# First loads, late value groups and half key products in the prologue of an attention and expert layer

## The reference

```python
q = x @ Wq + bq; k = x @ Wk + bk; v = x @ Wv + bv
q, k, v = (to_heads(q), to_heads(k), to_heads(v))        # 8 heads of 64
scores = jnp.einsum('bdsh,bdth->bdst', q, k) / SCALE
weights = jax.nn.softmax(scores, axis=-1)
feats = jnp.einsum('bdst,bdth->bdsh', weights, v)
x = _layernorm(x + (feats.reshape(B, S, F) @ Wo + bo))
# router: sigmoid(x @ w_gate), top 6 of 64 experts, places by a running count
# x_disp: the rows of x scattered to (expert, place), zero where no token stands
up = jnp.einsum('ecd,edh->ech', x_disp, w_up)
out_r = jnp.einsum('ech,ehd->ecd', silu(g_r) * v_r, w_down)
x = _layernorm(x + shared + routed)
```

## Time and profile before

| what | value |
|---|---|
| median of 3 runs | 1390.62 us (1387.7 to 1397.6) |
| the profiled execution | 1395.11 us, of which the span of the trace is 1393.3 us |
| busy share of the span | PE 92%, DVE 73%, ACT 65%, POOL 48% |
| prologue | 0 to 150.8 us in the trace |
| attention's first scores | 159.2 us |
| mean granted clock of TensorE | 0.974 of full speed |

### The profile page before, as it was taken

How to read it: one execution, slowest core, us unless ns; L and a number is a source line. 1 busy time by engine, 2 the same in 40 slices (tenths; PEclk the granted TensorE clock), 3 DMA queues, 4 the chain that set the end, 5 groups by cost and what they waited for, 6 DMA issues and landing times.

```text
span 1393.3 us, 24378 instructions
## 1 busy us (share of the span) xinstructions
PE 1280.9 (92%) x8129; PEld 1068.5 (77%) x8129; DVE 1017.0 (73%) x1879; ACT 901.2 (65%) x1639; POOL 664.8 (48%) x662
## 2 busy tenths in 40 slices
PE   6999799999999999999999999996678999999596
PEld 4888599899899899799799799796456767767332
DVE  4623488789799899799799789796445677677376
ACT  5411398878688688688688688686114666666242
POOL 0002122235636636636636636546363888888511
PEclk9999899999999999999999999998798999999899
DMA  6049966112423424324334333334455999997597
GB/s 232 0 186 353 344 215 217 55 37 86 136 70 129 130 86 137 105 86 137 112 95 129 121 102 127 108 107 140 157 204 171 335 353 346 347 359 274 208 419 303
DMA packets 155754, 252.78 MB, mean 181 GB/s; under 512 B 18660, under 2 KB 98916, under 8 KB 153201
## 3 DMA queue, kind: packets, MB, share of 16 engines
q1 hardware_dynamic: 130144, 192.19, 40.9%
q0 software_dynamic: 20992, 50.38, 9.5%
q10 hardware_dynamic: 4496, 8.65, 1.7%
HBM read 118.95 MB, written 134.33 MB: 182 GB/s over the span
## 4 chain that ended last, share of the span: by engine, by line
PE 66%; issue 12%; DMA 6%; SPq 4%; DVE 4%; POOL 4%; ACT 3%; another core or an unknown queue 2%; POOLq 0%; DVEq 0%; ACTq 0%
PE pv_acc L1256 13%; PE slot L1237 13%; PE slot L1224 12%; PE slot L1119 8%; PE slot L1333 4%; PE slot L1283 4%; PE misc L1170 4%; PE pv_acc L1119 4%; DMA got<-y_hbm 3%; SPq L397 3%; DVE rows_lo L1059 2%; ACT rows_hi L783 2%; PE slot L1355 1%; DMA moved<-scaled 1%
## 5 line engine op out<-in xcount | busy, mean ns | idle before, releaser
L740 ACT ACTIVATE p_hi<-slot 128x512 fp32r<-128x512 f32 x512 | 279.8, 596 | 108.6 <-PE slot L1224 86.4
L590 POOL TENSOR_TENSOR p_lo<-prob,p_hi 128x512 fp32r<-128x512 f32 x128 | 165.1, 1290 | 363.4 <-ACT prob L742 356.9
L1237 PE MATMUL slot<-k_stack,q_stack 128*128 128x512 f32 x1024 | 300.8, 416 | 8.5 <-DMA q_stack<-q_hbm 8.5
L753 ACT ACTIVATE prob<-prob,row_min 128x1024 f32<-128x1024 f32 x256 | 296.4, 1158 | 12.9 <-DVE prob L1035 12.9
L1014 DVE TENSOR_TENSOR p_lo<-slot,p_hi 128x512 fp32r<-128x512 f32 x384 | 251.3, 681 | 37.6 <-ACT p_hi L740 31.0
L1256 PE MATMUL pv_acc<-p_hi,v_pair 128*128 128x256 f32 x1024 | 265.6, 292 | 3.9 <-POOL p_lo L590 3.2
L1224 PE MATMUL slot<-ident,prob 128*128 128x128 f32 x2048 | 265.2, 272 | 1.2 <-ACT prob L753 1.2
L1256 PE MATMUL pv_acc<-p_lo,v_pair 128*128 128x256 f32 x1024 | 255.1, 282 | 0.0
L1224 PEld LDWEIGHTS slot<-ident,prob 128*128 128x128 f32 x2048 | 230.8, 140 | 1.7 <-DVE prob L1035 1.6
L1256 PEld LDWEIGHTS pv_acc<-p_hi,v_pair 128*128 128x128 f32 x1024 | 193.0, 189 | 18.0 <-issue 8.6
L1256 PEld LDWEIGHTS pv_acc<-p_lo,v_pair 128*128 128x128 f32 x1024 | 192.8, 188 | 11.7 <-issue 3.3
(11 more groups left out here) (142 smaller groups left out, 2092.4 us busy)
## 6 DMA issues: line engine op xcount, KB each, us to landing
disp_hbm<-zeros SPq DMA_DIRECT2D x64, 512.0 KB, 5.5
rows<-disp_hbm SPq DMA_DIRECT2D x64, 512.0 KB
y_hbm<-zeros SPq DMA_DIRECT2D x48, 512.0 KB
got<-y_hbm SPq DMA_DIRECT2D x16, 1536.0 KB, 11.9
q_stack<-q_hbm SPq DMA_DIRECT2D x128, 128.0 KB
up_w<-in_L_ffn_w_up SPq DMA_DIRECT2D x64, 256.0 KB
down_w<-in_L_ffn_w_down SPq DMA_DIRECT2D x32, 256.0 KB
q_hbm<-q_hi SPq DMA_DIRECT2D x8, 512.0 KB, 2.6
```

Of the source, the lines that this page charges most:

```text
L590: e.tensor_tensor(p_lo[1][:, 2:4, :], prob[:, m % 2, :, (4 * u + 2) * P:(4 * u + 4) * P], p_hi[1][:, 2:4, :].bitcast(F32), ALU.subtract).t ...
L740: e.activation(p_hi[b][:, two, :], view[:, two, :], ACT.Copy).then_inc(a_phi, 1)
L753: e.activation(keys, keys, ACT.Exp, bias=row_min[:, me % 2, j, 1:2], scale=-1.0, accum_out=row_sum[:, me % 2, j, half:half + 1]).then_inc( ...
L1237: made = e.matmul(slot[:, n * BANK:(n + 1) * BANK], qs[:, part, j * P:(j + 1) * P], k_stack[:, ms % H, keys], start=part == 0, stop=part == 1)
```

## The change

It has four parts. The first loads of q_stack (heads 0 and 1) are issued ahead of the zeroes, with a wait for the last query product (q_stack lies where the query weights were), and 24 of the zeroes stand in the prologue and 40 in the loop, where 32 and 32 did. The last two value groups are made behind the scores of steps 0 and 1, and DVE's part of them is placed between its steps 0 to 3. The first three key products are made by halves: the first half of all three, then the second half of all three. And PE, ACT and DVE wait for the constants alone (`constants_in`) ahead of attention, while PE waits for the value parts ahead of the first product with v_pair, in step 7; SP and POOL keep `prologue_over`. Three small tiles (row_min, row_sum, row_inv) move out of the memory that the prologue uses.

```diff
+        V_LATE = 2
         takes = [("k", n) for n in range(8)]
-        takes += [("q", n) for n in range(8)] + [("v", g) for g in range(NS)]
+        takes += [("q", n) for n in range(8)] + [("v", g) for g in range(NS - V_LATE)]
         for s in range(LAST + LAG):
             takes += ([("turn", s - LAG)] if s >= LAG else []) + ([("scores", s)] if s < LAST else [])
+            takes += [("v", NS - V_LATE + s)] if s < V_LATE else []
...
+        def constants_in(e):
+            e.wait_ge(g_const, 5)
+            e.wait_ge(d_fill, 16)
+            e.wait_ge(d_once, 32)
...
# SP
-            for g in range(E // 2):
-                e.dma_start(disp_pieces[g], zero_row).then_inc(d_zero, 16)
...
+            e.wait_ge(p_q, 8)
             load_q(0)
             load_q(1)
+            for g in range(Z_EARLY):
+                e.dma_start(disp_pieces[g], zero_row).then_inc(d_zero, 16)
             prologue_over(e)
...
-                if s < E // 2:
-                    e.dma_start(disp_pieces[E // 2 + s], zero_row).then_inc(d_zero, 16)
+                if s < E - Z_EARLY:
+                    e.dma_start(disp_pieces[Z_EARLY + s], zero_row).then_inc(d_zero, 16)
...
# DVE
+            for g in range(NS - V_LATE):
+                add_v(g)
+                if g < NS - V_LATE - 1:
+                    low_v(g)
+            constants_in(e)
...
+                if s < V_LATE:
+                    low_v(NS - V_LATE - 1 + s)
+                    add_v(NS - V_LATE + s)
+                elif s == V_LATE + 1:
+                    low_v(NS - 1)
...
# PE
-            for n in range(8):
+            for half in range(2):
+                for n in range(3):
+                    project("k", n, 0, n, 0, (half,))
+            for n in range(3, 8):
                 project("k", n, n // 4, n % 4, 0)
...
+            for g in range(NS - V_LATE):
+                make_v(g)
+            constants_in(e)
...
                     made.then_inc(p_scores, 1)
+                    if s < V_LATE:
+                        make_v(NS - V_LATE + s)
...
+                    if rv == 0:
+                        e.wait_ge(a_vhi, 2 * NS)
+                        e.wait_ge(v_vlo, NS)
+                        e.wait_ge(g_vlo, NS)
```

More of the change, by code:

```diff
@@ L109, in build @@
         count_so_far = sb("count_so_far", [P, E], BF16, att)
+        row_min = sb("row_min", [P, 2, QT, 2], F32, att)
+        row_sum = sb("row_sum", [P, 2, QT, 2], F32, att)
+        row_inv = sb("row_inv", [P, QT], F32, att)
         pro = ExitStack()
@@ L128, in build @@
         q_stack = [sb(f"q_stack{i}", [P, 2, QC], F32R, att) for i in range(2)]
-        row_min = sb("row_min", [P, 2, QT, 2], F32, att)
-        row_sum = sb("row_sum", [P, 2, QT, 2], F32, att)
-        row_inv = sb("row_inv", [P, QT], F32, att)
         scaled = sb("scaled", [P, QC], F32, att)
@@ L300, in build @@
         y_pieces = y_hbm.rearrange("(g p t) (u n) -> g p (t u) n", p=P, t=2, u=2)
-        NZ = T * TOPK // (2 * P)
+        NZ, Z_EARLY = T * TOPK // (2 * P), 24
         bv_all = wo_sb[:, 0, :]
@@ L700, in scalar @@
                                  ACT.Copy).then_inc(a_vhi, 1)
-            prologue_over(e)
+            constants_in(e)
             def flip_x1(c, j):
@@ L896, in vector, with add_v @@
             e.wait_ge(d_bv, 16)
-            for g in range(NS):
-                vp = v_plain[g % 2]
+            def add_v(g):
                 e.wait_ge(p_v, g + 1)
@@ L902, in vector, with low_v @@
                     e.wait_ge(g_vlo, g - 1)
-                e.tensor_tensor(vp[:, :, :], slot_of_take("v", g)[:, :].rearrange("p (t n) -> p t n", t=2),
+                e.tensor_tensor(v_plain[g % 2][:, :, :],
+                                slot_of_take("v", g)[:, :].rearrange("p (t n) -> p t n", t=2),
                                 bv_all.unsqueeze(1).to_broadcast([P, 2, C]), ALU.add).then_inc(v_vadd, 1)
+            def low_v(g):
                 e.wait_ge(a_vhi, 2 * g + 2)
-                e.tensor_tensor(v_pair[:, 2 * g + 1, :, D:P], vp[:, 1, :].rearrange("p (h c) -> p h c", h=H),
+                e.tensor_tensor(v_pair[:, 2 * g + 1, :, D:P],
+                                v_plain[g % 2][:, 1, :].rearrange("p (h c) -> p h c", h=H),
                                 v_pair[:, 2 * g + 1, :, 0:D].bitcast(F32), ALU.subtract).then_inc(v_vlo, 1)
-            prologue_over(e)
+            for g in range(NS - V_LATE):
[3 more added lines that the diff above has]
+            constants_in(e)
             def add_resid(c, j):
@@ L1122, in three_products, with project @@
                     made.then_inc(done, 1)
-            def project(name, n, g, pair, w):
+            def project(name, n, g, pair, w, halves=(0, 1)):
                 slot = slot_of_take(name, n)
@@ L1135, in project @@
                 cols = slice(pair * P, (pair + 1) * P)
-                for half in range(2):
+                for half in halves:
                     four = slice((2 * g + half) * 4, (2 * g + half + 1) * 4)
@@ L1148, in tensor, with make_v @@
             e.wait_ge(v_wlo, KC + 2)
-            for g in range(NS):
+            def make_v(g):
                 wait_bank(e, ("v", g), 0)
```

## The result

The changed kernel takes 1388.28 us (median of 20 runs), the kernel before 1395.63 us in the same comparison (20 runs): a ratio of 0.9952, with a 95% interval of 0.9938 to 0.9966, so 6.7 us faster (4.7 to 8.7). The forecast was 12.4 us, to 1378.2 us. The kernel before has a median 5.0 us above the one of three runs on which the forecast was built, which is why ratios are used from here on. The two traces have spans of 1393.3 and 1387.9 us.

What follows compares the result with a forecast made beforehand. PE was taken to bound attention, so time won ahead of it would stay won. The terms, 5.15 + 10.8 - 3.6 = 12.4 us, taken from 1390.62 us gave 1378.2 us, with a range of 1371 to 1386.

Steps and rivals of the forecast that it cites:

- What bounds the kernel: In attention PE is busy throughout; time is won only where PE stands still or runs slowly ahead of it.
- Part 1: Start of the kernel: key products by halves fill PE's 4.22 us without work, gaining 5.15 us (4.5 to 5.8).
- Part 2: Ahead of attention: first loads and late value groups bring the first transposes 10.8 us earlier (10.3 to 11.3).
- Part 3: Step 8: head 2's load follows SP's large wait, Wo and three zeroes, so PE waits 3.6 us (2.7 to 4.7).
- the sum: Whole kernel: 5.15 + 10.8 - 3.6 = 12.4 us faster, to 1378.2 us.
- The rival of the clock: At step 8's new wait the clock halves, costing 2.7 us: 9.7 us gained, 1380.9 us; chance 0.14.
- The other three rivals: Head 2's load in time, 1374.6 us, 0.12; key product reading holds PE, 1382.2, 0.05; queue never catches up, 1403.4, 0.02.

Runs made afterwards that it cites:

- the kernel with the large wait: Changed kernel with all value groups ahead of attention and the large wait on PE, ACT and DVE as before the change; ratio 0.993 to the kernel before, 9.6 us faster.

## Why the prediction was wrong

*What bounds the kernel, and that a us won ahead of attention stays won*: right. Four kernels with leads of 7.9, 14.8, 17.9 and 18.2 us at the first head have 8.4, 14.8, 17.5 and 22.5 at the last expert, and their timed gains, 7.0, 12.4, 14.9 and 16.2, follow at 1 to 3 us less.

*Part 1, the halves*: forecast 5.15 (4.5 to 5.8), measured 6.3 in the two traces and 7.0 by the timed runs of that part alone (4.5 to 9.3). The steps were right, as the rows of the changed kernel show that answer to the earlier trace rows:

```profile
12.70 0.63 PE L1141 MATMUL slot<-x_hi,w_lo 128*128 128x512 f32 x1
...
13.13 0.63 PE L1141 MATMUL slot<-x_hi,w_hi 128*128 128x512 f32 x1
13.56 0.63 PE L1141 MATMUL slot<-x_lo,w_hi 128*128 128x512 f32 x1
...
13.98 0.56 PE L1141 MATMUL slot<-x_hi,w_lo 128*128 128x512 f32 x1
...
14.38 0.40 PE L1141 MATMUL slot<-x_hi,w_hi 128*128 128x512 f32 x1
14.61 0.40 PE L1141 MATMUL slot<-x_lo,w_hi 128*128 128x512 f32 x1
```

No gap follows the last matmul of product 0's first half (12.70), and 3 slow matmuls do, where I had 1 to 7; from 14.38 the distance is 0.23. They stand 0.40 to 0.43 us apart, as the score matmuls of the kernel before do at a granted clock of 0.50 (four in 1.71 us, 161.07 to 162.78). The windows of the start show 1.00, so that the half clock there is read from the distances alone. Nothing waits for the reading of the key products. PE free at 13.13 and not at 13.47 is 0.3 us of the difference, and 0.2 the smaller number of slow matmuls. The last 0.5 is in the pace: the fast matmuls up to the end of group 5 stand 0.2328 us apart in the trace before and 0.2317 in this one, and there are over 500. The other traces have 0.231 to 0.233, so that is scatter and no merit of the change. With group 5 ending anywhere from 131.85 to 134.92, the gain would be 4.6 to 7.7 us against this one trace of the kernel before; a range of 4.5 to 5.8 was too narrow for it.

*Part 2*: forecast 18.3 us from value group 5 to the first transposes and a gain of 10.8, measured 18.29 and 10.85 (17.11 less 6.26). The order of DVE's list and the durations in the earlier trace rows carried this without a fault.

*Part 3, what the change leaves in its place*: this is the term that failed, "PE waits for 3.6 us". The mechanism and its place were right, and the ends, 2.7 to 4.7, were too near. The wait measured 6.8 us, with 1.95 of slow clock behind it, which the sum had at nothing. SP's wait fell at 150.89, 17.6 behind the end of group 5, as forecast. Two prices behind it were wrong.

The first is the rate. I sent Wo and the zeroes through the queue at 385 GB/s, the rate of zeroes in a queue that has been full for long, so that they had moved 25.2 us behind the end of group 5, at 158.4. By the windows their 2.62 MB had moved at 160.6. Of these 2.2 us, 1.5 were lost in the first 2 us and the rest from 154.5 to 157.0. Why the queue was slow there is not shown. Wo met an empty queue, but it is also a load, and no run separates the two. The kernel before has a stretch in which its queue is not empty, the loads of q_stack end and Wo begins, and the rate falls to 248 and 260 there:

```profile
156.50:157.00 0.50, 0.00 (x0) 0.00 (x0) 0.00 (x0) 0.00 (x0) 0.00 (x0) 0.50 1.11 293
157.00:157.50 0.50, 0.00 (x0) 0.00 (x0) 0.00 (x0) 0.00 (x0) 0.00 (x0) 0.50 1.26 248
157.50:158.00 0.50, 0.00 (x0) 0.00 (x0) 0.00 (x0) 0.00 (x0) 0.00 (x0) 0.50 1.48 260
```

So even the trace before had a row that spoke against 385 GB/s for loads.

The second is the landing. I let the load be in 2.2 us behind the bytes ahead of it: 1.3 to move, and 1 for its semaphore, which no run separates. (At the 133 to 168 GB/s that the text names, 0.26 MB takes 1.6 to 2.0 and not 1.3; and 27.4 less 23.7 is 3.7, not 3.6.) It took 3.0, from 160.6 to 163.6. By the windows 2.88 MB, which is Wo, three zeroes and the load, had moved by about 161.3, and by the time the load was in, nearly 0.9 MB of the zeroes issued behind it had moved too. That fits engines that don't go in step, with a load that is in when the last of them has its share; but it is read from sums of bytes, and no run isolates it.

The estimate by the Trainium skill's fixed 2.0 us and 436 GB/s (DMA: Bandwidth & Descriptors, Anatomy of one DMA), a wait of 2.6 us, was further off still. The page gives that fit for a single transfer issued by GpSimd, and the trace disagrees with it for SP's transfers, which queue.

*The rival of the clock* held 0.14 as an alternative to a wait of 3.6 us. It was no separate case but belonged into the sum: with a wait of 6.8 us the clock fell, as in the earlier trace rows. In the traces with waits of 1.1 to 2.2 us it stayed. The price I gave, 2.7 us, was for 24 slow matmuls in a row; here it was 1.95. The other three rivals didn't happen: PE doesn't wait for the reading of the key products, it waits for no later load of q_stack, and the load of head 2 isn't in time.

The sum with the measured terms is 6.3 + 10.8 - 6.8 - 1.95 = 8.4 us at the first head, against 6.7 (4.7 to 8.7) timed. Without the 5.2 us that the wait and the clock cost beyond the forecast 3.6, it would have been 13.5, 1.1 over the forecast, and that is part 1's excess.

## What to carry to other kernels

When a load is moved ahead of a block of transfers, look at the next load behind it: here the first two were freed and the third stayed behind a wait for everything, where making work late pushed it 2 us further back while the engine that needs it came 17 us sooner. Price a wait on a shared queue by what stands ahead of it, and take the rate from a row with the same kind of transfer and the same state of the queue, empty or full; here the rate of a steady stream of zeroes was too kind to a load into an empty queue. If a wait is near the length at which the clock fell in the trace, put the slow clock into the range of the main case. And a part of a change that looks good in the schedule can be worth less than nothing until one line elsewhere is moved: late value groups cost 5.7 us here (5.0 in the traces), and in the traces are worth 2.3 once the load is in time.

## What the runs showed of the hardware

A 1 MB load into a queue that had been empty for some 7 us moved at 131, 131, 16 and 115 GB/s in its first four half us (131, 115, 131 and 197 in a second kernel), while the stores of the queries, into a queue empty for 2.5 us in the kernel before, moved at 270 and 401 in their first two. The two differ in direction and in how long the queue was empty, and no run tells which of them matters. The granted clock fell from 2.4 to 1.2 GHz after PE had been idle for about 4.0 us (157.15 to 161.1), 3.6 us in the kernel before, 2.7 in the halves alone (143.4 to 146.1) and only 2.1 us in the kernel with the large wait (146.3 to 148.4); it stayed up in waits of 1.1, 1.5 and 2.2 us. The Trainium skill (TensorE: Matmul & The Clock Gate, What's actually happening) has the chip look at PE in windows that run freely; the four different idle times agree with that, and a length of waiting that is safe can't be read from one trace.
